# A chain moved earlier in each strip, and two evictions moved behind the first scores

## The reference

```python
x = x + _layernorm(attn(_layernorm(x)))        # attn: q, k, v = projections of 1024 features
#   scores = q @ k.T / 32;  masked = where(causal, abs(scores), -inf)
#   out = softmax(masked) @ v;  attn = out @ Wo.T + bo
x = x + _layernorm(ffn(_layernorm(x)))         # ffn: x @ int4(kernel) + bias + (x @ a) @ b
```

## Time and profile before

| what | value |
|---|---|
| median of 3 runs | 3802.57 us (3717.16 to 3941.55) |
| the profiled execution | 3719.82 us |
| its span on the slowest core (core 1) | 3718.1 us |
| span of the eight cores | 3692.8 to 3718.1 us |
| mean granted TensorE clock | 0.876 (core 1) |
| TensorE busy | 2700.5 us, 73% of the span |
| VectorE busy | 1364.8 us, 37% |
| ScalarE busy | 1408.4 us, 38% |
| the first phase B, by its first and last rl | 665.9 to 1852.5 us |

### The profile page before, as it was taken

How to read it: one execution, slowest core, us unless ns; L and a number is a source line. 1 busy time by engine, 2 the same in 40 slices (tenths; PEclk the granted TensorE clock), 3 DMA queues, 4 the chain that set the end, 5 groups by cost and what they waited for, 6 DMA issues and landing times.

```text
span 3718.1 us, 57317 instructions; the slowest of 8 cores (3692.8 to 3718.1 us)
## 1 busy us (share of the span) xinstructions
PE 2700.5 (73%) x17129; PEld 1635.8 (44%) x17129; DVE 1364.8 (37%) x2102; ACT 1408.4 (38%) x3137; POOL 406.1 (11%) x728
## 2 busy tenths in 40 slices
PE   2279987566777777888846988946667778778884
PEld 1233333333445555566613433323444455556661
DVE  3334554344344333333333112024443443333333
ACT  0055453223333344444415555422333344434441
POOL 0000001000011111111100000000011111111110
PEclk9999999778788998999957999967878898999996
DMA  5622222222222333333304222132132233333330
GB/s 147 197 91 91 97 77 99 91 69 63 85 86 83 94 98 113 106 111 114 103 35 153 74 74 69 61 118 68 43 105 81 89 94 94 120 103 109 114 103 23
DMA packets 96559, 348.16 MB, mean 94 GB/s; under 512 B 16245, under 2 KB 16373, under 8 KB 94858
## 3 DMA queue, kind: packets, MB, share of 16 engines
q0 software_dynamic: 64112, 226.54, 19.5%
q1 hardware_dynamic: 32154, 117.97, 9.7%
HBM read 266.85 MB, written 77.59 MB: 93 GB/s over the span
## 4 chain that ended last, share of the span: by engine, by line
PE 49%; DVE 21%; ACT 16%; issue 8%; DMA 4%; ACTq 1%; DVEq 1%; POOLq 0%; SPq 0%; POOL 0%
PE SBp L491 11%; PE SBp L872 7%; PE OTp L532 6%; PE OTp L913 6%; DVE sqb L195 6%; DVE stats L192 6%; PE EB L752 4%; PE LBp L752 4%; PE EB L640 3%; PE LBp L640 2%; DVE t L662 2%; ACT Sa L880 2%; DVE sqb L216 2%; ACT stats L201 2%; ACT stats L203 2%
## 5 line engine op out<-in xcount | busy, mean ns | idle before, releaser
L913 PE MATMUL OTp<-PT,V_buf 128*128 128x256 bf16 x4352 | 608.9, 286 | 274.7 <-ACT PT L893 273.7
L872 PE MATMUL SBp<-Qs,Ktr 128*128 128x256 bf16 x4352 | 621.8, 291 | 225.4 <-DVE rl L609 177.0
L913 PEld LDWEIGHTS OTp<-PT,V_buf 128*128 128x128 bf16 x4352 | 432.7, 102 | 380.9 <-issue 313.9
L872 PEld LDWEIGHTS SBp<-Qs,Ktr 128*128 128x128 bf16 x4352 | 416.1, 103 | 352.0 <-issue 272.5
L491 PE MATMUL SBp<-lnT,wsl 128*128 128x512 bf16 x2048 | 484.2, 401 | 77.1 <-ACT Qs L498 44.3
L932 POOL DMA_DIRECT2D Ktr<-k_scr x544 | 297.9, 548 | 1917.4 <-PE SBp L872 1836.7
L208 DVE TENSOR_TENSOR stats<-stats 128x1 f32<-128x1 f32 x256 | 40.7, 159 | 921.3 <-ACT stats L206 908.9
L491 PEld LDWEIGHTS SBp<-lnT,wsl 128*128 128x128 bf16 x2048 | 207.3, 102 | 348.6 <-issue 135.1
L880 ACT ACTIVATE Sa<-SBp 128x256 f32<-128x256 f32 x544 | 209.2, 385 | 379.5 <-PE SBp L872 347.9
L192 DVE TENSOR_REDUCE stats<-t 128x1 f32<-128x1024 f32 x160 | 195.2, 1220 | 298.9 <-ACT t L767 278.4
L893 ACT ACTIVATE PT<-Sa 128x256 bf16<-128x256 f32 x544 | 227.1, 418 | 166.8 <-ACT Sa L880 91.4
(11 more groups left out here) (110 smaller groups left out, 2764.8 us busy)
## 6 DMA issues: line engine op xcount, KB each, us to landing
Ktr<-k_scr POOLq DMA_DIRECT2D x544, 256.0 KB, 2.9
xb<-x SPq DMA_DIRECT2D x128, 512.0 KB, 3.7
y<-xb POOLq DMA_DIRECT2D x64, 512.0 KB, 3.8
q_scr<-Qs POOLq DMA_DIRECT2D x32, 512.0 KB, 5.0
k_scr<-Ktr POOLq DMA_DIRECT2D x64, 256.0 KB, 2.9
Qs<-q_scr SPq DMA_DIRECT2D x32, 512.0 KB, 5.5
xb<-fk SPq DMA_DIRECT2D x8, 512.0 KB, 5.8
xb<-wo SPq DMA_DIRECT2D x8, 512.0 KB, 6.2
```

Of the source, the lines that this page charges most:

```text
L872: E("tensor", lambda e, j=j, dc=dc, sp=sp, qof=qof: e.matmul(out=SBp[:, sp * 512:sp * 512 + 256], lhsT=Ktr[:, (j % 4) * 1024 + dc * 128:(j ...
L913: lst=(last and vc % 2 == 1): e.matmul(out=OTp[b_][:, col:col + 256], lhsT=V_buf[:, j * 1024 + vc * 128:j * 1024 + (vc + 1) * 128], rhs=PT ...
```

## The change

Two entries of the hand-written table are edited.

- The evictions of the first two `OTp` banks move from `pre` to `pre2`. All four are now emitted behind the absolute value and exponential of the next strip's first tile; before, two were emitted ahead of that strip's first scores and two behind.
- `lnffn_chain(0)` moves in `main` from factor 0.97 to 0.84.

```diff
-                for b_ in range(2):
-                    pre.append(t_otevac(b_))
-                pre2 = [t_otevac(2), t_otevac(3)]
+                pre2 = [t_otevac(b_) for b_ in range(4)]
...
                 main.append((0.80, lnattn_b(1)))
-                main.append((0.97, lnffn_chain(0)))
+                main.append((0.84, lnffn_chain(0)))
                 spill.append((0.04, ln2t_pe(1)))
```

## The result

The changed kernel takes 3837.07 us (median of 10 runs, 3828.57 to 4000.43) beside 3755.71 us (10 runs, 3716.92 to 3941.55) for the kernel before. The medians count every execution, also those in which a die ran at a lower clock; the ratio leaves these out: 1.0308, interval 1.0286 to 1.0329. Of the 3720 us at which the forecast was made that is 115 us more, where 56 were forecast. 3837 lies outside the range, which ended at 3825.

A forecast was written before the change was run, and what follows sets the result against it. TensorE's waits for L609's reciprocal (177.0 us) and L893's exponential (273.7 us) were taken as bounding; large -5.5, small +19, middle +11, starts +31, ends +1 gave +56 on 3719.8, so 3776 us, range 3712 to 3825.

The forecast's parts named there:

- The end gap and the new stall: At nt = 28, the strip-end gap shrinks from 6.5 to 1.0 us; a 3.7 us stall appears behind LNattn_b(1).
- Part 1: Strip ends: the chain's move from 0.97 to 0.84, priced by strip size at -5.5, +19 and +11 us.
- large, small and middle strips: Switches at nt = 22 to 30 (10, -5.5 us), 8 to 14 (8, +19) and 16 to 20 (6, +11).
- The two ends of a phase: No strip follows; the longer ScalarE queue ahead of L709 costs what the earlier chain gives: +1 us in both.
- Part 2: Strip starts: four L617 evictions behind the first exponential, 1.38 us more on ScalarE; +31 us, bounds 0 and 41.
- Starts 16.6 + 9 + 5 = +31: Eviction cost in us at 12 starts up to nt = 14, 8 at 16 to 22, 10 at 24 to 32.
- the worst case: Each of 24 switches comes 2.7 us later and the evictions cost 41: +106 us, 3826 us.
- One in two: Share of new large-strip stalls followed by 3.4 us at half clock, costing 1.7; so +0.85 us each.
- four in five: Share of new stalls followed by low clock above which the forecast's case of slower by over 2% decides.
- slower by over 2%: the stall brings the low clock with it: Rival: each mid-strip stall brings 1.7 to 3.4 us more in 24 strips, about +50; 3825 us; 20%.
- Near zero: the clock pays: Rival: clock stays at 2.4 GHz at all large and middle switches, evictions cost half; 3735 us; 22%.
- the faster way: Rival: the strip-end gap goes and no stall comes, a gain of 120 us less evictions; 3600 to 3640; 5%.

The follow-up runs named there:

- e1: Kernel before with only the lnffn_chain(0) move from 0.97 to 0.84, evictions as before; ratio 1.0075 to the kernel before, +28 us.
- e10: Kernel before with the chain at 0.84 only in strips nt = 22 to 32, 0.97 elsewhere, evictions as before; ratio 0.9991 to the kernel before.
- e2: Changed kernel with the chain put back to 0.97, all four evictions behind the first exponential; ratio 1.0204 to the kernel before, +76 us.
- e4: Changed kernel plus zero matmuls (14, or 26 below nt = 20) ahead of the stalled values product, nt 16 and more; ratio 1.0217 to the kernel before.

## Why the prediction was wrong

**The end gap and the new stall: right.** 3.63 us at nt = 28 and a gap of 1.14, a wait for L609 of 61.3 us (58 foretold) and for the exponential of 399 (380).

**Part 1 by groups: right in small and middle strips, right by luck in large ones.** Foretold -5.5, +19 and +11 for large, small and middle strips, together +24.5 (+25.5 with the ends). e1 alone gives -6.8, +21.2 and +11.1; by its ratio it costs 28. That the mask add would be late in small strips was most of it, and the rows of nt = 8 show it step by step. The -5.5 of the large strips was made of 10 x -1.4 of standing and 10 x 0.85 of clock, and neither term came so. Behind their first four key tiles the standing fell by 12.4 us (14 foretold), but the low time at work rose by 29.1, which costs 14.5 and not 8.5. In the first four tiles the low time at work fell by 42.0, worth 21, for which part 1 had nothing, while TensorE stood 8.5 us more there: at nt = 28 the first values product now waits 0.81 us for the exponential, where before it waited for nothing. The misses go opposite ways, and the sum came out near. "The two ends of a phase", put at +1 for both parts, were low as well: +7.2 in e1 and +8.4 in e10 up to the last product. What lies behind it gives back 4.4 and 1.6, about as much as the stretch ahead of the first strip, in which nothing was changed, differs by in these two profiles (4.1 and 3.0). The strip nt = 32 has the same new stall of some 3.7 us, once in each phase, and the text charged it only for ScalarE's queue.

**Part 2: the step that failed.** "Starts 16.6 + 9 + 5 = +31", with "bounds 0 and 30 x 1.38 = 41 us". Alone it measured 76. The reasoning followed ScalarE's queue and found its delay nearly: TensorE stands 40 us more, 30 x 1.34. It took the move as a delay only, and for the large strips trusted that the clock would pay for part of it. But the 1.38 us fall on TensorE as pieces of idleness cut into its busy start, and the clock is at 0.50 for 58 us more with TensorE at work, worth 29; the account leaves 5 us unexplained. For this the forecast had no term, and the upper bound was no bound, since it left the clock out; for the same reason the whole change, +115, is above what the forecast called the worst case, +106. By groups of starts the account of e2 gives +31 for nt up to 14 (16.6 foretold), +18 for 16 to 22 (9) and +25 for 24 to 32 (5): where I charged least, and counted on the clock, I missed by most.

**What the parts do to each other** had no term. The accounts put it at about 12 us of the 115, mostly at nt = 16 to 20, but that is within the intervals of the ratios, and no run isolates it.

**The clock behind the new stalls.** "One in two" for large strips was wrong. Of the 80 new stalls at nt = 22 to 30 (five strips, two phases, eight cores) 78 in e1 and 73 in the changed kernel are followed by more than 1 us at 0.50 within the next 3.4. That is over the "four in five" at which the slow case was said to decide. The low time of nt = 22 to 30 as a whole, 3.9 us under before in the changed kernel, hides it, since the short gap gives low time back in the same strips.

**The clock behind the short gap.** In e1 the mean granted clock in the first 2 us of the strips nt = 22 to 30 is 0.97, where it is 0.50 before. The rule of the Trainium skill (TensorE: Matmul & The Clock Gate, "What's actually happening"), by which the throttled state is the default and activity releases it, named this, and the traces agree. Of the 10 x 1.7 = 17 us that the forecast estimated by it, the first four tiles show 21 in e1, less the 8.5 of standing. In e2, where the long gap stays, the evictions add 26 us of low time at work to the same tiles, and in the changed kernel they take back most of what the gap gave (-7.0 instead of -42.0).

**The rivals.** The case "slower by over 2%: the stall brings the low clock with it" (3825, 20%) was nearest in the number, in part by luck. The low clock did follow the new stalls, and filling them gives 34 us back in e4 (22 by the account). But the short gaps gave at least as much back in the large strips, and the chain as a whole cost about what was forecast. What was missed is the low clock at the starts behind the moved evictions, 29 us by the account of e2, and that case did not name it. "Near zero: the clock pays" fell, as did the faster way for this place of the chain.

## What to carry to other kernels

On an engine that works in order, an instruction that waits for another engine belongs where nothing behind it is urgent: against its old place at 0.97 the same chain costs 28 us more at 0.84, and 116 us less behind the next strip's first tile. Work that lies hidden in a gap costs more than its length when it is moved out of it. A short wait of TensorE is to be priced twice, once for its standing and once for the clock behind it, and the second price depends on where the wait falls: moving the chain alone brought 29 us of standing and no clock in sum, moving the evictions alone 40 us of standing and 29 of clock. Only low time in which TensorE has work counts.

## What was not expected of the hardware

That pieces of 0.3 to 1.1 us of idleness between pairs of matmuls can be followed by a granted clock of 0.50, just as one stall of 3.63 us is: 0.66 over the first 15 us of a strip in e2, with 12.06 us of them busy, against 0.81 and 13.37 busy before. The amount of idleness doesn't decide it alone, since in e1 TensorE is busy for 12.18 us of the same 15 and the clock is 1.00; what does is open. And that matmuls with zero weights count as work: with 26 of them in a stall of 6.3 us the next product took 1.03 us instead of 1.87.
